# A decoder layer on one core: attention's probabilities turned by VectorE in 32 by 32 blocks, and five output products in flight

## What is computed

```python
q, k, v = (x @ Wq), (x @ Wk), (x @ Wv)          # 16 heads of 64; q and k get rotary factors
logits = jnp.einsum('bhqd,bhkd->bhqk', q, k)
logits = jnp.where(causal, logits, MASK_VAL) / jnp.sqrt(jnp.float32(HEAD_DIM))
attn = jax.nn.softmax(logits, axis=-1)
out = jnp.einsum('bhqk,bhkd->bhqd', attn, v)
x = _layernorm(x + out @ Wo)
# then: x = _layernorm(x + cross_attention(x, ctx)); x = _layernorm(x + ffn(x))
```

## Time and profile before

| | |
|---|---|
| median of three runs | 540.87 us (540.30 to 541.53) |
| the profiled execution, its own time | 540.99 us |
| span of its trace | 539.2 us |
| PE busy | 530.3 us, 98% of the span |
| DVE busy | 288.5 us, 54% |
| ACT busy | 242.6 us, 45% |
| POOL busy | 156.3 us, 29% |
| granted clock of TensorE | 0.999 of full speed |

### The profile page before, as it was taken

The page is one execution under the profiler, slowest core; times in us unless marked ns, Lnnn a source line. Parts: engine busy times, 40 slices in busy tenths (PEclk is TensorE's granted clock), DMA queues, the critical chain, the costliest instruction groups (busy, mean ns, idle before and its releaser), DMA issues.

```text
span 539.2 us, 7875 instructions
## 1 busy us (share of the span) xinstructions
PE 530.3 (98%) x2996; PEld 456.5 (85%) x2996; DVE 288.5 (54%) x560; ACT 242.6 (45%) x567; POOL 156.3 (29%) x139
## 2 busy tenths in 40 slices
PE   8999999999999999999999999999999999999995
PEld 6888889999999998999988889888787888888884
DVE  5810000264555647374633676788996776855432
ACT  5703201054454454553435636365776656535231
POOL 0004500643353535554003440021957110101010
PEclk9999999999999999999999999999999999999999
DMA  9906622511101111100059647569879466523011
GB/s 287 309 2 175 176 55 63 176 60 68 41 25 65 41 40 41 39 2 1 1 174 253 155 112 194 159 191 258 254 213 284 128 179 191 144 57 103 33 63 55
DMA packets 37957, 65.60 MB, mean 122 GB/s; under 512 B 4872, under 2 KB 20616, under 8 KB 37920
## 3 DMA queue, kind: packets, MB, share of 16 engines
q1 hardware_dynamic: 37392, 64.84, 41.7%
q10 hardware_dynamic: 528, 0.26, 0.2%
HBM read 54.08 MB, written 3.67 MB: 107 GB/s over the span
## 4 chain that ended last, share of the span: by engine, by line
PE 92%; DMA 3%; POOL 2%; DVE 1%; ACT 1%; SPq 1%; issue 0%; POOLq 0%; ACTq 0%
PE bank L532 30%; PE bank L659 26%; PE bank L543 14%; PE bank L741 5%; DMA half_raw<-ffn_w 3%; PE bank L557 3%; PE bank L584 3%; PE bank L571 2%; PE bank L770 2%; PE bank L772 2%; PE bank L775 2%; PE bank L617 1%; PE bank L714 1%; POOL ffn L1728 1%; PE bank L725 1%; PE bank L790 1%
## 5 line engine op out<-in xcount | busy, mean ns | idle before, releaser
L532 PE MATMUL bank<-x_hi,w_hi 128*128 128x448 f32 x256 | 95.3, 372 | 0.0
L532 PE MATMUL bank<-x_lo,w_hi 128*128 128x448 f32 x256 | 94.0, 367 | 0.0
L532 PE MATMUL bank<-x_hi,w_lo 128*128 128x448 f32 x256 | 94.0, 367 | 0.0
L1699 POOL TENSOR_TENSOR w_lo<-w_mix,w_hi 128x1024 fp32r<-128x1024 f32 x16 | 38.1, 2379 | 115.2 <-ACT w_hi L918 115.2
L659 PE MATMUL bank<-wo,act_hi 128*128 128x512 f32 x224 | 70.4, 395 | 0.0
L659 PE MATMUL bank<-ffn,act_hi 128*128 128x512 f32 x224 | 69.9, 393 | 0.0
L1712 POOL TENSOR_TENSOR norm<-norm,minus_half 128x1 f32<-128x1 f32 (+1 forms) x22 | 15.8, 720 | 159.0 <-DVE norm L1403 159.0
L933 ACT ACTIVATE prob<-prob,shift 112x112 f32<-112x112 f32 x128 | 47.8, 376 | 24.6 <-DVE shift L1345 24.6
L532 PEld LDWEIGHTS bank<-x_hi,w_hi 128*128 128x128 f32 x256 | 48.1, 188 | 5.2
L532 PEld LDWEIGHTS bank<-x_hi,w_lo 128*128 128x128 f32 x256 | 48.1, 188 | 4.7
L532 PEld LDWEIGHTS bank<-x_lo,w_hi 128*128 128x128 f32 x256 | 48.1, 188 | 4.3
(11 more groups left out here) (115 smaller groups left out, 1020.6 us busy)
## 6 DMA issues: line engine op xcount, KB each, us to landing
cf_raw<-ctx_feat SPq DMA_DIRECT2D x32, 376.0 KB, 4.4
ct_raw<-ctx_tok SPq DMA_DIRECT2D x24, 448.0 KB
w_raw<-qkv_w SPq DMA_DIRECT2D x16, 512.0 KB, 3.4
half_raw<-wo_w SPq DMA_DIRECT2D x16, 256.0 KB, 6.6
half_raw<-ffn_w SPq DMA_DIRECT2D x16, 256.0 KB, 6.9
wv_raw<-qkv_w SPq DMA_DIRECT2D x15, 256.0 KB, 7.1
x_raw<-x_feat SPq DMA_DIRECT2D x7, 448.0 KB, 7.9
out<-y_t SPq DMA_DIRECT2D x6, 512.0 KB, 4.4
```

The costliest lines, as they stand in the source:

```text
L532: last = pe.matmul(to[:, 0:HT], a[:, k, :], b[:, k, HT * h:HT * h + HT], start=(k == 0 and b is x_hi and a is w_hi[w]), stop=(k == KT - 1 ...
L1699: pool.tensor_tensor(w_lo[w][:, :, :], w_mix[:, :, :], w_hi[w][:, :, :].bitcast(F32), ALU.subtract).then_inc(w_rest, 1)
```

## The change

- **Turning.** TensorE's 16 transposes per step (`turn_prob` on PE) and ACT's four copies (`keep_prob_t`) go. DVE turns instead: `prob` and `prob_t` become two wide tiles each of 128 partitions (rows beyond 112 cleared once, by four memsets of 128 x 912, `cleared`), and one DVE instruction (STREAM_TRANSPOSE) turns one 32 by 32 block of all eight matrices of a half. Keys after the query are masked, so 10 of the 16 block positions suffice: 10 instructions per half, 20 per step, in parts of five (`turn_prob(p, r, part)`).
- **Dividing.** `normalise` moves from DVE (four instructions of 448 columns) to ACT (16 instructions of 112 columns, each with its row's inverse as a scale read per partition). DVE keeps the reciprocals (`invert`).
- **Maximum.** The score scale moves into the mask addition (SCALAR_TENSOR_TENSOR) and the sign into the reduction (`negate=True`); the four small TENSOR_SCALARs per step go.
- **Order in a step.** TensorE projects four k slices instead of three before it scores, and scores before it mixes. ACT starts with the exponentials and rounds the heads after the first half. DVE takes both halves' maxima first, and the parts of `turn_prob` stand between the four `keep_qk`.
- **Behind the loop.** `GROUPS` swaps its fourth and fifth entry, six banks are given to the first six groups, and group (3, 0) is computed in the free time of the last pair beside the three and beside (0, 1): five groups are begun before the first whole one. The last half of the last pair has a bank of its own. `turn_tile(0)` moves into the middle of `wo(2, 1)`.
- **Later.** The order of loads on SP, of rounding on ACT, of rests on DVE and POOL changes by a place or two at some twenty points; no instruction is added or removed there.

```diff
-GROUPS = ([(0, 0), (1, 0), (2, 0), (3, 0), (0, 1), (1, 1), (2, 1), (4, 0), (5, 0), (3, 1), (6, 0),
+GROUPS = ([(0, 0), (1, 0), (2, 0), (0, 1), (3, 0), (1, 1), (2, 1), (4, 0), (5, 0), (3, 1), (6, 0),
...
-        GROUP = [bank[0], bank[7], bank[1], bank[4]] + [bank[g % 2] for g in range(2 * WO - 4)]
+        GROUP = [bank[b] for b in (0, 7, 1, 5, 4, 6)] + [bank[g % 2] for g in range(2 * WO - 6)]
...
-                for k in range(3):
+                for k in range(4):
                     project_part(k, 0, 0, PROD[0])
+                score(p, up, 0)
+                pe.wait_ge(qk_kept, 4 * p + 4)
+                score(p, up, 1)
                 if p:
                     mix_heads(p - 1, 0)
                     mix_heads(p - 1, 1)
-                pe.wait_ge(qk_kept, 4 * p + 4)
-                score(p, up, 0)
-                score(p, up, 1)
-                for k in range(3, KT):
+                for k in range(4, KT):
                     last = project_part(k, 0, 0, PROD[0])
...
                 project(1, 1, PROD[1])
-                turn_prob(p, 0)
-                turn_prob(p, 1)
...
             three(0, (0, 1))
+            score(s, 1, 0)
             pe.wait_ge(qk_kept, 4 * s + 4)
-            pe.wait_ge(prob_t_kept, 4 * s)
-            score(s, 1, 0)
             score(s, 1, 1)
             three(0, (2,))
+            three(1)
             mix_heads(p, 0)
-            three(1)
+            three(2)
+            three(3)
             mix_heads(p, 1)
-            for k in range(2, 6):
-                three(k)
-            turn_prob(s, 0)
+            three(4)
+            three(5)
             pe.wait_ge(heads_rest, 2 * last_p + 1)
             three(6)
-            turn_prob(s, 1)
+            pe.wait_ge(masked, 4 * s + 4)
+            for k in range(KT - 1):
+                if k == 6:
+                    pe.wait_ge(heads_rest, 2 * last_s)
+                three(k, (4,))
             mix_heads(s, 0)
-            pe.wait_ge(masked, 4 * s + 4)
+            pe.wait_ge(wo_rest, NB + 4)
             for k in range(4):
                 three(k, (3,))
-            mix_heads(s, 1)
             pe.wait_ge(heads_rest, 2 * last_s + 1)
             three(7)
+            mix_heads(s, 1)
...
-            def keep_prob_t(p, r):
+            def normalise(p, r):
                 for h in range(2):
                     a = 2 * r + h
-                    act.wait_ge(prob_turned, 4 * p + a + 1)
-                    if any_yet(2 * (p - 1) + r + 1):
-                        act.wait_ge(heads_done, 2 * (p - 1) + r + 1)
-                    act.activation(prob_t[a][:, :, :], turn_bank(p, r)[h][0:S, 0:HT],
-                                   ACT.Copy).then_inc(prob_t_kept, 1)
+                    act.wait_ge(inverted, 4 * p + a + 1)
+                    for b in range(HB):
+                        last = act.activation(prob[a][:, b, :], prob[a][:, b, :], ACT.Copy,
+                                              scale=inv[:, a, b:b + 1])
+                    last.then_inc(normed, 1)
...
+            def quads(wide, rows, cols):
+
+                return bass.AP(wide, QUAD * rows * WIDE + QUAD * cols, [[WIDE, QUAD], [S, 2 * HB], [1, QUAD]])
+
+            def turn_prob(p, r, part):
+
+
+                def block(key, query):
+                    return dve.transpose(quads(prob_t_wide[r], key, query),
+                                         quads(prob_wide[r], query, key))
...
             def step(s, u):
                 p = s - 1
...
+                mask_and_top(p, 0)
+                mask_and_top(p, 1)
+                invert(p, 0)
                 if p:
                     rest_heads(p - 1, 0)
...
                     rest_heads(p - 1, 1)
...
                 keep_qk(u, 0, 0, 4 * s + 1, PROD[0])
-                normalise(p, 0)
+                turn_prob(p, 0, 0)
                 keep_qk(u, 0, 1, 4 * s + 2, PROD[1])
-                normalise(p, 1)
+                invert(p, 1)
+                turn_prob(p, 0, 1)
                 keep_qk(u, 1, 0, 4 * s + 3, PROD[0])
+                turn_prob(p, 1, 0)
                 keep_qk(u, 1, 1, 4 * s + 4, PROD[1])
...
+                turn_prob(p, 1, 1)
...
-            load_ff(3)
-            load_cf(15)
+            load_cf(16)
...
             add_one(0)
             add_one(1)
-            add_one(2)
             rest_ff(0)
             power(0, 4, P)
             rest_ff(1)
+            add_one(2)
+            add_one(3)
```

254 lines of the change are left out of this document (131 added, 123 removed).

## The result

The changed kernel takes 525.75 us (median of six runs, 523.76 to 526.46) against 540.45 us for the kernel before (six runs, 539.24 to 541.53). The ratio on record is 0.9715, with a 95% interval of 0.9700 to 0.9731; the quotient of the two medians is 0.9728, inside it. The medians differ by 14.7 us. The later run e6 had a fifth execution of 789.98 us at a granted clock of 0.611 (0.979 or more in all others here); it isn't in e6's median, and since e6's trace is of that execution, e13 repeats e6.

A forecast was written before the change was run, and what follows sets the result against it. TensorE, busy 530.3 of 539.2 us, was taken as the bound: 540.99 - 12.3 (transposes) - 0.8 (waits) = 527.9 us, 527.8 against the median. Its own range was 526.3 to 529 (chance 0.72); a wider one was 526.2 to 532 (some 0.85).

The forecast's parts named there:

- What bounds, and what goes from TensorE: Loop and last pair: TensorE bounds, so removing its transposes, 1.54 us a step, saves 12.3 us in all.
- Everything else on TensorE has the same count ... are only moved: Scores, heads and output-group matmuls on TensorE: same count, only reordered, so counted as no gain.
- TensorE's two waits: Waits for the context rows' rests: 1.6 us in two; between nothing and 1.6 us won, 0.8 taken.
- rival (a): Masks, behind the loop, loads: small waits eat part of the gain, costing 1 to 5 us, 529 to 533; chance 0.16.
- DVE: Loop step: 20 turning blocks of 0.42 us each make 17.5 us of DVE work in 23.44 us, ready in time.
- ACT: Loop step: 16 scalings at 0.29 us each bring ACT to 14.5 us of 23.4, so it isn't full.
- The spare behind that: DVE in a loop step: it would be full only at 0.72 us a turning block, by its busy times.
- The five groups in flight are worth nothing by themselves: Behind the loop: they only cover the last pair's softmax; without the fifth, some 5.0 us of TensorE would be bare.
- The second tile: Behind the loop: its norm would be 1.4 us late in the old order; with the new order no wait counted.
- Rival (b): DVE's turning contends with POOL; TensorE stands up to 2.6 us a step at the heads, 547 us; chance 0.06.
- Rival (c): DVE's turning blocks are slow, 0.949 us each, giving 28.0 us a step and 562 us; chance 0.03.
- Rival (d): Loop: TensorE loses the transposes but waits as long for turned tiles through ACT and DVE; 540 to 541 us; chance 0.03.

The follow-up runs named there:

- e6: The changed kernel without the fifth output group in flight, its 24 matmuls done in one piece behind the other four; 525.92 us.
- e13: The changed kernel with four output groups in flight instead of five, run once more for its trace; 525.04 us.
- e5: The changed kernel with 16 unused transposes of the identity put back at the end of each step on TensorE; 536.45 us.
- e12: The changed kernel with TensorE's entire old sequence in a step, 16 unused transposes included, other engines keeping their new work; 538.14 us.
- e1: The kernel before with the scores ahead of the heads in a step on TensorE; 538.43 us.
- e9: The changed kernel with two neighbouring calls on DVE exchanged, mask_t(0) ahead of rest_cf(22); 524.01 us.
- e10: The changed kernel with 30 or 40 turning blocks a step in place of 20; 530.99 us with 30, 564.21 us with 40.
- e14: The changed kernel with the old order at the second tile: turn_tile(0) ahead of wo(2, 1), POOL's second power behind rest_low, round_low earlier on ACT; 528.45 us.
- e3: The kernel before with one more unused 112 by 112 transpose between the scores and the projections of each step; 541.65 us.
- e7: The kernel before with four slices of the projection, not three, ahead of heads and scores; 538.52 us.
- e8: The changed kernel with heads ahead of scores and three slices of the projection in front, not four; 527.67 us.
- e2: The changed kernel with the heads ahead of the scores in a step, as before; 524.19 us.

## Why the prediction was right in its mechanism and wrong in its sum

- **What bounds, and what goes from TensorE: right.** 12.3 us for 128 transposes; the loop's chain without them and e5 with them give 1.54 us a step.
- **"Everything else on TensorE has the same count ... are only moved": this step failed.** The count was the same and the time was not: 7 x 0.34 = 2.4 us less, by the distance of the projections' starts. The prediction took 0.209 us a matmul from the chain of before (18.17 / 87) for the time of any such matmul; it belongs to the slow rhythm. e12 shows that the old sequence brings it back, e1 that the kernel before could have been rid of it by a reordering alone: 538.43 us against 540.68, without any turning on DVE. What in a sequence sets the rhythm stays open.
- **TensorE's two waits: mis-sized.** Both went, as the upper bound had it (1.6 us), but a new one of 1.5 us came at L682, of the kind named under rival (a). Instead of 0.8 us 0.1 was left over. The two errors have opposite signs, 2.4 us too little won and 0.7 too much, and the miss looks smaller than its larger part by that luck. With the wait taken out as in e9, the sum of prediction and rhythm is 540.18 - 12.3 - 2.4 - 1.6 = 523.9 us from the kernel before timed beside it, and e9 took 524.01.
- **DVE: right.** 0.436 us a block against 0.42. Its 17.1 us a step had been put at 17.5; the last turning ended 0.5 us ahead of the masks against 0.7.
- **ACT: right.** 0.28 us a scaling against 0.29.
- **The spare behind that: too large.** 0.72 us a block came from DVE's busy sum. The ring through ACT leaves 0.66 by the estimate from e10, since DVE can't turn while it waits for the first half's exponentials.
- **"The five groups in flight are worth nothing by themselves": right; "some 5.0 us would be bare": wrong.** Without the fifth group TensorE asks 5 us earlier and still doesn't wait (e13). The walk had the second tiles ready 1.5 us before they were wanted, and so they are. What it had wrong is that this time is fixed: the last turning is queued behind a rest that waits 4.59 us for TensorE's own heads, so it comes sooner when they do.
- **The second tile: right that no wait came, and the price of the old order low:** 1.4 us said, 2.4 us of waits at the two tiles in e14, 1.1 of them at the second.
- **Rival (b), contention: refuted** by 2.24 us for five blocks beside POOL and away from it. **Rival (c), slow blocks: refuted** by 436 ns; e10 with 40 blocks is that rival made real, a single run, slower than before by 24 us. **Rival (d): refuted**, TensorE has no wait in the loop. **Rival (a)** happened once, at 1.5 us, and was hidden by the rhythm.

The low end of 526.2 held both old waits gone and cheap scalings. The waits alone lead to 540.87 - 12.3 - 1.6 = 527.0 us; for the other 0.7 us no path was given by which cheaper scalings on ACT would shorten TensorE's chain. It held nothing for the part that was counted at zero because it was only moved.

## What to carry to other kernels

When TensorE is the bound, work that others can do in time is worth its own length in TensorE's chain, and the walk through the other engines' queues, instruction by instruction, says whether they are in time better than their busy sums do. Where an edit reorders TensorE, compare the distance of starts in its long runs, before and after: here a reordering alone was worth 2.3 us (e1). When the bound engine has become 12 us earlier, look at every join behind it: tiles, rests and masks that were just in time can be late then, and a swap of two neighbours in a queue mends them (e9, e14). When a time in a walk hangs on the bound engine itself, let it move with that engine before you pay for cover (e13).

## What the runs showed of the hardware

- A long run of 448-column fp32r matmuls at full granted clock has two rhythms here, one start every 206.7 ns or every 202.7 ns. Changing what TensorE did ahead of it changed the rhythm (e1, e3, e7, e8), changing the other engines' work didn't (e12). The same matmuls in a step can have either (e7, e8), and what decides is open.
- DVE's STREAM_TRANSPOSE of 32 x 256 fp32 takes 0.436 us on average, five in 2.24 us, and POOL's two-input work beside it doesn't slow it. A subtraction with both inputs in SBUF on DVE was slowed from 0.94 to 3.12 us (e9 and after, L1506). The Trainium skill (SBUF — State Buffer, Who interferes with whom) names two-input instructions as contending and single-input ones not; both measurements agree, and the turning, which its list lacks, behaves like the single-input ones.
- In that contention the one that starts second waited. POOL 0.22 us ahead: DVE's subtraction took 3.12 us and POOL's two instructions 2.54 (after). DVE 0.05 us ahead: 0.93 us and 3.28 (e2).
- The granted clock fell to half for 3.4 us right behind a wait of TensorE of 2.6 us (e10 with 30 blocks, 409.1 to 412.5); behind the wait of 1.5 us in after it stayed full, and behind some waits of 2.7 us in e10 with 40 blocks too.
